# Head pairs, shared key features and a later graph softmax in the second attention of a GNN block

## The reference

```python
# attention: 16 heads of 64, 266 random features (proj is 266 x 64)
def _softmax_kernel(data, proj, is_query):
    ratio = proj.shape[0] ** (-0.5)
    dn = data.shape[-1] ** (-0.25)
    dash = einsum('bhnd,md->bhnm', data * dn, proj)
    diag = 0.5 * dn ** 2 * sum(data * data, axis=-1, keepdims=True)
    stab = max(dash, axis=-1) if is_query else max(dash, axis=(-2, -1))
    return ratio * (exp(dash - diag - stab) + EPS)
q, k, v = (split_heads(x @ W) for W in (Wq, Wk, Wv))
qp = _softmax_kernel(q, proj, True)
kp = _softmax_kernel(k, proj, False)
k_sum = sum(kp, axis=2)
d_inv = 1.0 / einsum('bhnm,bhm->bhn', qp, k_sum)
context = einsum('bhnm,bhnd->bhmd', kp, v)
out = einsum('bhnm,bhmd,bhn->bhnd', qp, context, d_inv)
return merge_heads(out) @ Wo + bo
# graph attention: 10625 edges, 4 heads of 64
e = einsum('ehd,hd->eh', leaky_relu(xl[src] + xr[dst]), att)
p = exp(e - segment_max(e, dst)[dst])
alpha = p / (segment_sum(p, dst)[dst] + 1e-16)
out = segment_sum(alpha[..., None] * xl[src], dst).reshape(n, 256) @ W_up
```

## Time and profile before

| | |
|---|---|
| median of 3 runs | 1915.22 us |
| lowest, highest | 1914.4, 1917.06 us |
| the profiled execution, its own time | 1917.35 us |
| its span | 1915.5 us |
| mean granted clock of PE | 0.969 |
| PE busy (matmul) | 1796.1 us, 94% |
| DVE, ACT, POOL busy | 730.6, 389.9, 666.1 us |

### The profile page before, as it was taken

The page is one execution under the profiler, slowest core; times in us unless marked ns, Lnnn a source line. Parts: engine busy times, 40 slices in busy tenths (PEclk is TensorE's granted clock), DMA queues, the critical chain, the costliest instruction groups (busy, mean ns, idle before and its releaser), DMA issues. The chain is left out here.

```text
span 1915.5 us, 22173 instructions
## 1 busy us (share of the span) xinstructions
PE 1796.1 (94%) x8594; PEld 1142.6 (60%) x8594; DVE 730.6 (38%) x1491; ACT 389.9 (20%) x715; POOL 666.1 (35%) x571
## 2 busy tenths in 40 slices
PE   7999999998999999998999989999989899999953
PEld 5466446444545777556777756577644576676731
DVE  5966112323525231463455565421301223222226
ACT  0000000001411010002677635111000312222222
POOL 0676881030000186777888500000440222222210
PEclk9999999998999999999899999999989899999986
DMA  9545124172620153333222162150511699999952
GB/s 351 171 111 143 2 23 133 40 222 46 247 93 5 41 150 102 94 94 86 53 55 56 23 168 84 66 222 1 150 44 44 231 409 412 402 413 408 404 156 85
DMA packets 104071, 289.12 MB, mean 151 GB/s; under 512 B 61941, under 2 KB 65239, under 8 KB 91836
## 3 DMA queue, kind: packets, MB, share of 16 engines
q1 hardware_dynamic: 28634, 224.83, 31.8%
q0 software_dynamic: 68160, 51.85, 12.2%
q10 hardware_dynamic: 7198, 11.36, 1.9%
HBM read 257.19 MB, written 30.32 MB: 150 GB/s over the span
## 5 line engine op out<-in xcount | busy, mean ns | idle before, releaser
L325 PE MATMUL bank<-wring,turned_a 128*125 128x512 f32 x480 | 207.6, 593 | 1.6 <-DVE turned_a L640 0.7
L523 POOL DMA_INDIRECT table_d<-wring x85 | 174.2, 2050 | 94.7 <-issue 64.3
L886 POOL DMA_INDIRECT wring<-xl_d,wring x85 | 108.7, 1278 | 258.7 <-DMA xr_d<-flat_b 232.8
L325 PEld LDWEIGHTS bank<-wring,turned_a 128*125 128x125 f32 x480 | 89.6, 188 | 115.3 <-issue 114.2
L2138 PE MATMUL bank<-picked_t,wring 128*128 128x128 f32 x1280 | 148.0, 278 | 7.4 <-ACT picked_t L2385 7.4
L2138 PEld LDWEIGHTS bank<-picked_t,wring 128*128 128x128 f32 x1280 | 146.1, 195 | 14.9 <-ACT picked_t L2385 7.6
L341 PE MATMUL bank<-flat_d,wring 128*128 128x312 f32 (+1 forms) x512 | 135.0, 426 | 0.0
L899 POOL DMA_INDIRECT score_d<-wring x85 | 108.3, 1274 | 69.4 <-DMA score_d<-wring 45.8
L886 POOL DMA_INDIRECT wring<-xr_d,wring x85 | 111.7, 1314 | 25.9 <-issue 24.1
L341 PEld LDWEIGHTS bank<-flat_d,wring 128*128 128x128 f32 x512 | 96.7, 189 | 37.9
L2153 PE MATMUL bank<-wring,unit_t 128*128 128x512 f32 x160 | 74.0, 605 | 0.0
(11 more groups left out here) (433 smaller groups left out, 2778.9 us busy)
## 6 DMA issues: line engine op xcount, KB each, us to landing
wring<-in_experts SPq DMA_DIRECT2D x60, 2048.0 KB, 14.2
wring<-in_L_Ws SPq DMA_DIRECT2D x6, 2048.0 KB, 17.8
table_d<-eq_buf SPq DMA_DIRECT2D x2, 3072.0 KB, 30.1
score_d<-no_edge SPq DMA_DIRECT2D x2, 3072.0 KB, 33.5
wring<-table_d POOLq DMA_DIRECT2D x10, 610.4 KB, 7.3
wring<-score_d SPq DMA_DIRECT2D x5, 1093.8 KB
wring<-pid_d ACTq DMA_DIRECT2D x17, 312.5 KB
wring<-in_edge_w ACTq DMA_DIRECT2D x17, 312.5 KB
```

The costliest lines, as they stand in the source:

```text
L325: ins = pe.matmul(bank[0:R, :], act_t[:, k, tok(t)], w[:, k * HALF:(k + 1) * HALF], start=(k == 0), stop=(k == chunks - 1))
L523: pool.indirect_dma_start(out=tables_d[b % 2], out_offset=bass.IndirectOffsetOnAxis(ap=edge_at[:, b:b + 1], axis=0), in_=edge_sums[:, b, : ...
L886: pool.indirect_dma_start(out=to[:, g % 2, j, :], out_offset=None, in_=table, in_offset=bass.IndirectOffsetOnAxis(ap=index[:, b:b + 1], ax ...
```

## The change

The loop now takes a pair of heads and a node tile in one step, 40 key slots and 40 query slots in 53 steps; queries start at step 12 and outputs at step 13.

- The 80 products for maxima beside the values are gone. The loop's own key products are taken with the row maxima at once (`k_top`; keys are stored negated, so it is a minimum), the exponential subtracts the row's maximum, and once the pair's overall maximum is known each feature is scaled by `k_scale` = exp(row maximum - head maximum - diagonal) and gets EPS added. A ring of 18 feature tiles holds them meanwhile. `ratio` is dropped.
- Square sums use 64-column weights, two in the two column halves of the array, and move 313 and 312 nodes. Those of the keys stand beside the values GEMM, those of the queries in the loop.
- The context is made the other way round: the values (64 columns per head) are the weights, the two heads of a pair in the two halves of the array, and the 266 features move past. A second such product with ones makes the sums. DVE and ACT copy it out and PE transposes it per pair. The last ten features of both heads share one piece of 20.
- Outputs are normalised and transposed slot by slot in the loop, so the turning after it is gone.
- Edge groups stand at other places: 5 and 6 beside the values, 7 to 14 at fixed steps of the loop, 15 and 16 at the tiles 0 and 3 of the output GEMM.
- The softmax of the graph no longer stands between the tiles of the output GEMM. Maxima of tiles 0 and 1 stand at its tiles 6 and 7, all else follows it, and the up product goes tile by tile.

```diff
-        V_GROUP_AT = {1: 5, 3: 6, 6: 7, 8: 8}
+        V_GROUP_AT = {1: 5, 5: 6}
+        LOOP_GROUPS = {7: 3, 8: 10, 9: 18, 10: 23, 11: 29, 12: 34, 13: 39, 14: 47}
+        O_GROUP_AT = {0: 15, 3: 16}
+        Q_AT, O_AT = 12, 13
+        STEPS = SLOTS_K + O_AT
+        FEAT_AT = {2: (0,), 3: (1, 2), 4: (3, 4)}
+        CTX_AT = {3: (1, (0,)), 4: (1, (1, 2)), 0: (2, (3, 4))}
...
+                for u in range(STEPS):
+                    q, phase, pair = u - O_AT, u % T, chain_of(u)
+                    if 0 <= q < SLOTS_K:
+                        pe.wait_ge(hsem["q_exp"], 2 * q + 2)
+                        turn_queries(q, range(4), banks[6])
...
+                        query_slot(u - Q_AT)
+                    if 0 < q <= SLOTS_K:
+                        turn_output(q - 1)
+                    key_a, key_b = k_banks(u)
+                    if k_last_use(u) >= 0 and u <= SLOTS_K:
+                        pe.wait_ge(hsem["k_exp"], 2 * k_last_use(u) + 2)
...
+                    if u < SLOTS_K:
+                        for i, bank in enumerate((key_a, key_b)):
+                            rows_i = slice(i * DH, (i + 1) * DH)
+                            pe.matmul(bank[0:R, 0:M], k1_t[rows_i, u // T, tok(u % T)], proj[rows_i, :],
+                                      start=True, stop=True).then_inc(hsem["k_prod"], 1)
+                    if 0 <= q < SLOTS_K:
+                        if q:
+                            pe.wait_ge(hsem["o_step"], 2 * q)
+                        turn_queries(q, (4,), banks[7])
...
+                            for w in range(2):
+                                for i in range(2):
+                                    values = v1[:, t, (2 * p + i) * DH:(2 * p + i + 1) * DH] if w == 0 else ones[0:R, 0:DH]
+                                    ins = pe.matmul(banks[4 + w][i * DH:(i + 1) * DH, 0:M], values,
+                                                    kf[:, (2 * at + i) % RING_U, :], start=(t == 0), stop=(t == T - 1))
+                            ins.then_inc(hsem["k_used"], 1)
...
+                    if 0 <= q < SLOTS_K:
+                        outputs(q)
+                turn_output(SLOTS_K - 1)
...
-                pe_gemm_rows(pe, k1_t, beside=attend)
-                sring.wait_empty(pe)
-                pe_gemm_slot(pe, gat_t, 2)
...
+                for t in range(T):
+                    turn_probs(t)
+                    if t:
+                        gat_rows(t - 1)
+                    if t >= 2:
+                        up_product(t - 2)
+                gat_rows(T - 1)
+                up_product(T - 2)
+                up_product(T - 1)
...
+                for t in range(T):
+                    weigh(t)
+                    if t + 2 < T:
+                        find_tops(t + 2)
+                    if t >= 3:
+                        add_up(t - 3)
+                for t in range(2, T):
+                    add_up(t)
```

More of the change, by code:

```diff
@@ L871, in gps_kernel @@
         sq = carve(2 * N, rows=P).rearrange("p (s n) -> p s n", s=2)
[L872 to L873 removed]
+        sums = carve(N, rows=P)
         gathered = [sem("gathered_0"), sem("gathered_1")]
@@ L993, in gps_kernel, with k_banks, k_last_use, by_head @@
         gat_marks = {}
+        def k_banks(step):
+            return banks[2:4] if step < Q_AT and step % 2 else banks[0:2]
+        def k_last_use(step):
+            return step - 2 if step <= Q_AT else step - 1
+        def by_head(values):
+            return values.rearrange("f j (i d) -> f j i d", i=2)
+        def chain_of(step, back=1):
+            pair = step // T - back
+            return pair if 0 <= pair < K else None
         with nc.Block() as block:
@@ new lines, in outputs @@
+                def outputs(q):
+                    p = q // T
+                    if q % T == 0:
+                        pe.wait_ge(hsem["ctx_kept"], 2 * p + 2)
+                    pe.wait_ge(hsem["q_feat"], 2 * q + 2)
+                    for j, (f0, f) in enumerate(CH):
+                        ins = pe.matmul(banks[7][0:R, R:R + 2 * HEAD_W], qf_t[0:f, j, :], context[0:f, p % 2, j, :],
+                                        start=(j == 0), stop=(j == 4))
+                    ins.then_inc(hsem["q_used"], 1)
@@ new lines, in squares_of, with feature @@
+                def squares_of(buf, c):
+                    if c >= 2:
+                        s.wait_ge(squares_used, c // 2)
+                    squared.mark(s.activation(sq[:, c % 2, :], buf[:, c % K, :], ACT.Square))
+                for c in range(K):
+                    squares_of(k1_t, c)
+                s.wait_ge(pool_set, EPS_COL)
+                def feature(dst, src):
+                    return s.activation(dst, src, ACT.Identity, bias=eps_col[0:src.shape[0], 0:1])
+                for u in range(STEPS):
+                    phase, pair, p = u % T, chain_of(u), chain_of(u, 2)
+                    q = u - O_AT
+                    if 0 <= q < SLOTS_K:
+                        s.wait_ge(hsem["q_turned"], 2 * q + 1)
+                        feature(qf_t[:, 0:4, :], banks[6][:, 0:4 * R].rearrange("f (c r) -> f c r", r=R))\
+                            .then_inc(hsem["q_feat"], 1)
+                        s.wait_ge(hsem["q_turned"], 2 * q + 2)
+                        feature(qf_t[0:BOTH, 4, :], banks[7][0:BOTH, 0:R]).then_inc(hsem["q_feat"], 1)
+                    q = u - Q_AT
+                    if 0 <= q < SLOTS_K:
@@ new lines, in _ @@
+                        for i in range(2):
+                            s.activation(qf[:, q % 2, i * M:(i + 1) * M], banks[2 + i][0:R, 0:M], ACT.Exp,
+                                         bias=q_bias[:, q % 2, i:i + 1]).then_inc(hsem["q_exp"], 1)
+                    if u < SLOTS_K:
+                        for i, bank in enumerate(k_banks(u)):
+                            h = 2 * (u // T) + i
+                            s.wait_ge(hsem["k_top"], 2 * u + i + 1)
+                            if i == 0 and 2 * u >= RING_U:
+                                s.wait_ge(hsem["k_used"], u - RING_U // 2 + 1)
+                            s.activation(kf[:, (2 * u + i) % RING_U, :], bank[0:R, 0:M], ACT.Exp, scale=-1.0,
+                                         bias=neg_top[:, u % T, h:h + 1]).then_inc(hsem["k_exp"], 1)
@@ new lines, in _ @@
+                    if pair is not None and phase == 1:
+                        heads = slice(2 * pair, 2 * pair + 2)
+                        s.wait_ge(chain_step, 3 * pair + 3)
+                        s.activation(k_scale[:, :, heads], k_scale[:, :, heads], ACT.Exp).then_inc(hsem["k_scaled"], 1)
+                    if pair is not None:
+                        for t in FEAT_AT.get(phase, ()):
+                            at = pair * T + t
+                            part = kf[:, (2 * at + 1) % RING_U, :]
+                            s.wait_ge(hsem["k_scaled"], pair + 1)
+                            s.wait_ge(hsem["k_exp"], 2 * at + 2)
+                            s.activation(part, part, ACT.Identity, scale=k_scale[:, t, 2 * pair + 1:2 * pair + 2],
+                                         bias=eps_col[0:R, 0:1]).then_inc(hsem["k_feat_b"], 1)
```

551 lines of the change are left out of this document (302 added, 249 removed).

## The result

The changed kernel takes 1923.87 us (median of 20 runs, 1915.96 to 1934.71), the kernel before 1916.45 (20 runs, 1911.93 to 1921.12). The ratio is 1.0045, 95% interval 1.0032 to 1.0058: slower by 7.4 us. I had said 1893 and faster; the range ended at 1922.

A forecast was written before the change was run, and what follows sets the result against it. PE's own list and its waits were taken to bound the kernel. Values -45.9, loop +14.4, turning -5.2 and after the loop +14.6 sum to -22.1, from 1917.35 to 1895.2, stated as 1893 us; range 1873 to 1922.

The forecast's parts named there:

- Values to loop: Stretch from the start of the values to the feature loop: 78.2 us instead of 124.1, so -45.9.
- The turning: Turning of the feature loop's outputs, after the loop: it goes away, -5.2 us.
- X + 22: After the loop: first turning of probabilities 22 us after X, the moment the scores are in, put at 1134.7.
- my 218: Forecast length in us of the whole feature loop, against 203.6 before: +14.4.
- Outputs are five pieces instead of six, 0.69 x 5/3 = 1.15: Loop, PE's work: output products of a joint step take 1.15 us, scaled from the earlier trace's 0.69.
- The last 13 have queries only: End of the loop: 13 steps without keys, product to output following one another, 3.85 us each, 50 us.
- The clock of the key steps: Loop's first 12 steps, keys only: PE taken to run at 1.2 GHz until queries join, costing about 5 us.
- the term of the softmax, +14.6: Output GEMM and softmax after the loop: 145.0 us instead of 130.4, with DVE leading once the scores are in.
- Rival 2: Joint steps lose overlap, 6.1 us each, loop 252, time 1927; decides from 5.7 us a step; chance 0.12.
- Rival 3: Softmax behind the output GEMM runs at half clock, five tiles end 42 us later, time 1935; chance 0.07.
- Rival 1: Loop overlaps better, 205 us or less, and POOL bounds; time 1880; chance 0.17.
- rival 4: Whole kernel: the parts cancel within what can be told, 0.2% or 3.8 us; chance 0.05.

The follow-up runs named there:

- e5: Changed kernel with e2's full 128-row last feature piece and e1's bias load ahead of the scores: 1900.74 us, ratio 0.9922 to the kernel before.
- e1: Changed kernel with the output bias load issued before the wait for the last scatter, ahead of score and count loads: 1912.76 us, ratio 0.9972 to the kernel before.
- e4: e3 with e1's bias load ahead of the scores added: 1915.74 us, ratio 0.9977 to the kernel before.
- e6: e5 with the step reordered: query and key products together, then fifth turning and the previous output's turning, context, outputs: 1889.92 us, ratio 0.9860 to the kernel before.
- e9: e6 plus one unread 128-row-deep product per joint step, between 64-row query and key products: 1895.91 us, ratio 0.9884 to the kernel before.
- e10: e6 plus one unread product per joint step, 64 rows deep like its neighbours, same columns as e9: 1892.64 us, ratio 0.9864 to the kernel before.
- e12: e1 plus three unread products a step in the loop's last seven steps, to hold the clock: 1914.21 us, ratio 0.9971 to the kernel before.
- e3: e2 with all five query-feature turnings first, then query and key products, context, previous output's turning, outputs: 1927.30 us, ratio 1.0051 to the kernel before.
- e2: Changed kernel with the last 20 features turned and multiplied as a whole piece of 128 rows: 1915.23 us, ratio 0.9989 to the kernel before.
- e8: e5 plus unread products: three a step in the loop's last seven steps, 42 before the first probability turning: 1902.81 us, ratio 0.9931 to the kernel before.
- e11: e6 with the last edge groups and first weighing placed earlier, as in e7: 1889.41 us, ratio 0.9847 to the kernel before.
- e7: e5 with edge groups 14 to 16 and the first weighing placed earlier: 1897.32 us, ratio 0.9891 to the kernel before.

## Why the prediction was wrong

**What was right.** Values to loop: -45.9 predicted, -48.6 measured (by the marks of the trace; no experiment took this part by itself). Column halves at 0.94 ns a column held: two context tiles take 1.94 us (953.49 to 955.43). The turning: -5.2. The kernel's last stretch counted from the scores: X + 22 for the first turning, X + 22.3 in e5; 145.0 us long, 142.3 to 145.4 in e1, e4, e5 and e6. The scores were to be in at 1134.7; in e5, whose loop is 10 us longer than my 218, it was 1140.3, and in e6, with a loop of 218.7, 1131.0.

**The step that failed first: "Outputs are five pieces instead of six, 0.69 x 5/3 = 1.15".** I scaled groups of the earlier trace rows by their number of products. A group's time is its columns plus the changes of shape at its edges, 0.20 us each (e9 against e10), and the new step has up to eight such changes where two steps before had four. The outputs were 1.50 instead of 1.15, the six transposes with their places between products of other shape 1.04 instead of 0.75. PE's list of 4.4 us a step was 5.0, so a joint step averaged 5.18 (145.0 for 28) where I had 4.9, and its two longest kinds 5.8 and 5.9, above the 5.7 that I had named as the point at which the forecast falls. The Trainium skill, "TensorEngine Tiling (Array Packing)", section "Key Properties", states that a change of tiling mode, not of the tile alone, drains the engine. The traces agree in that such a change costs time, 0.20 us. The rows before showed the sign: 0.65 us for two pairs of products side by side, of 266 columns each, where e6 shows such pairs 0.55 apart if the next is of their own shape. That is one half of the price; the other half falls inside the group behind (e9's product holds PE 0.41 us, 990.86 to 991.27, for 0.22 of columns).

**The second: "The last 13 have queries only ... 3.85 each".** The context of the last pair is made until step 46. Steps 40 to 46 took 5.2 each (36.3 us in all, 1.6 of it the stretch at half clock in step 42), and only the last six were 4.2. That is 9.4 us, most of it a misread of the code's lags. The last six, where PE waits about 0.46 us twice a step, for DVE and for ACT, make 2.0 more.

**The clock of the key steps: right in sum by luck.** I had 25 us for the twelve steps of keys alone and 5 more because they would run at 1.2 GHz. They took 30.4, but at 2.4 GHz for the most part (windows of PE in the changed kernel):

```profile
860.00:870.00 10.00, 7.24 (x45) 0.98 0.29 63
870.00:880.00 10.00, 9.11 (x68) 1.00 0.24 54
880.00:890.00 10.00, 5.63 (x31) 0.71 0.24 53
```

So the steps themselves were 5.4 us longer than I had them, with 8.8 us of waits among them, and most of the clock's 5 was not paid. In e12's profiled run, where the clock was 0.57 from 860 to 880, the same steps took 34.3.

The loop's 18.9 us are thus 8.0 in the 28 joint steps, 9.4 and 2.0 behind them, and 5.4 in the key steps, less the 6 that I had put down for the clock and the end.

**The third: the term of the softmax, +14.6, was +24.2.** Its chain was right and its start was wrong: "From X DVE leads", with the bias as one more sum on the way. I priced the sum and not the load behind it. SP's order put it last, DVE's order put it first. It cost 13 to 14 us of the stretch (e1 with its half clock put right, e4 against e3, e5 against e2).

**The rivals.** Rival 2 came nearest, with 1927 us and joint steps above 5.7, but that is luck. It named waits (DVE's normalising) as the cause and 6.1 us for every step. In the changed kernel PE waited only 4.4 us in the 28 joint steps and worked through changes of shape. e3 has a wait of the kind that rival 2 described, and its loop is 12 us longer than e2's. Rival 3 (softmax at half clock) didn't decide: e8. Rival 1 was far off, and the change is larger than the 0.2% of rival 4.

With the first and third mended, the loop is 218.7 us and the kernel 1889.92 in e6, ratio 0.9860; e11's 1889.41 can't be told from it. That this loop is as long as my 218 is chance, since its list and its waits are others. Of e6's 34 us over the changed kernel (35 by the ratios), 11 to 14 are the bias, 9 to 11 the last piece, and 11 to 12 the order.

## What to carry to other kernels

When you price TensorE's list by rows of another order, price the columns and the changes of shape apart: count how often the part of the array in use changes from one group to the next. For each new wait on a vector engine, read what stands ahead of it in that engine's queue and, if it is a load, what stands ahead of the load in the issuing queue; both ends have to be read, since either alone looks harmless. And when steps are staggered by lags, list which steps still carry which part before you multiply by a count.

## What the runs showed of the hardware

- A change between products of 64 rows and of 125 to 128 rows costs 0.20 us on TensorE at 2.4 GHz (1.71 against 1.30 us for two, with equal columns). One between 128 and 20 rows costs 0.17: without two of them the outputs take 1.21 instead of 1.50 us and the four turnings behind them 0.52 instead of 0.58 (e2). A product of 128 rows is no dearer than one of 20.
- Ten fp32 records of 130 columns with full-depth weights go at 0.11 us each; their weight loads of 125 columns stay hidden.
- Two DMA scatters of one GpSimd queue of which the second waits for the first to land follow each other at 2.8 us (e5 and e7).
